# Fourth layer of a four-block transformer: key pieces ordered by VectorE and ScalarE in place of GpSimd

## The reference, cut to what matters

```
# layers 1 to 3:  scores[b,h,n,m] = q[b,h,n,:] . k[b,h,m,:]         (over tokens)
# layer 4:        attn = einsum('nthd,ntkd->nthk', q * scale, k)     (over heads, for each token)
#                 out  = einsum('nthk,ntkd->nthd', softmax(attn), v)
#                 out  = out.transpose(0, 2, 1, 3).reshape(n, t, d)
```

## Time and profile before

| | us |
|---|---|
| median of the three timed runs | 1486.37 |
| the profiled execution | 1485.1 |
| its span in the profile | 1483.4 |
| PE busy in the span | 1256.1 |
| DVE busy | 1121.3 |
| ACT busy | 935.5 |
| POOL busy | 325.4 |

### The profile page before, as it was taken

How to read it: one execution, slowest core, us unless ns; L and a number is a source line. 1 busy time by engine, 2 the same in 40 slices (tenths; PEclk the granted TensorE clock), 3 DMA queues, 4 the chain that set the end, 5 groups by cost and what they waited for, 6 DMA issues and landing times.

```text
span 1483.4 us, 36868 instructions
## 1 busy us (share of the span) xinstructions
PE 1256.1 (85%) x13282; PEld 808.8 (55%) x13314; DVE 1121.3 (76%) x2839; ACT 935.5 (63%) x2107; POOL 325.4 (22%) x446
## 2 busy tenths in 40 slices
PE   6365779888869999999999999999878898888886
PEld 4122335655446666666666666666645565656654
DVE  3844668877778888888888888888868888897642
ACT  0032456657637777777777777777657777776763
POOL 2000111111122222222222222222233343333301
PEclk9996688999979999999999999999989999999998
DMA  6304444234424444444444454444599999999900
GB/s 183 102 0 105 114 107 111 74 72 120 115 75 116 126 128 126 126 125 127 124 125 126 125 127 124 126 124 126 122 94 130 96 124 137 143 136 114 89 26 24
DMA packets 198481, 163.63 MB, mean 110 GB/s; under 512 B 80136, under 2 KB 182480, under 8 KB 192160
## 3 DMA queue, kind: packets, MB, share of 16 engines
q1 hardware_dynamic: 189920, 153.60, 54.5%
q10 hardware_dynamic: 8384, 7.69, 1.8%
HBM read 98.05 MB, written 62.41 MB: 108 GB/s over the span
## 4 chain that ended last, share of the span: by engine, by line
PE 36%; DVE 20%; DMA 12%; ACT 11%; issue 11%; SPq 6%; ACTq 3%; another core or an unknown queue 0%; DVEq 0%; POOL 0%; POOLq 0%
PE lin L1515 7%; PE lin L1531 6%; DMA norm_room<-stack_dram 5%; DMA stack_room<-stack_dram 4%; DVE maxima L1120 4%; PE o_bank L1468 4%; ACT hT_last L713 3%; PE score_bank L1406 3%; ACT p_room L732 3%; PE score_bank L1362 2%; PE st_bank L1437 2%; ACT h2T L718 2%; ACT h1T L718 2%; DVE gated L1178 2%; SPq L421 2%
## 5 line engine op out<-in xcount | busy, mean ns | idle before, releaser
L1120 DVE TENSOR_REDUCE maxima<-score_bank 128x4 f32<-128x512 f32 x512 | 329.1, 684 | 109.1 <-PE score_bank L1406 107.6
L732 ACT ACTIVATE p_room<-st_bank 128x512 f32<-128x512 f32 x512 | 276.9, 598 | 117.5 <-PE st_bank L1437 87.9
L616 POOL TENSOR_TENSOR part_low<-qk_rest,part_mid 96x512 bf16<-96x512 f32 x96 | 111.2, 1158 | 405.5 <-DVE part_mid L1103 405.5
L1531 PE MATMUL lin<-w_f,gelu 128*128 128x144 f32 (+1 forms) x1280 | 181.2, 299 | 3.8 <-ACT max_T L815 2.5
L1531 PEld LDWEIGHTS lin<-w_f,gelu 128*128 128x128 f32 (+1 forms) x1280 | 171.6, 201 | 7.3 <-ACT max_T L815 3.7
L1515 PE MATMUL lin<-h2T,w_h 128*128 128x512 f32 (+1 forms) x320 | 170.6, 632 | 4.4 <-ACT h2T L718 2.6
L1406 PE MATMUL score_bank<-stack_room 62*128 62x128 bf16 x2048 | 104.5, 223 | 77.3 <-DMA stack_room<-stack_dram 34.1
L1468 PE MATMUL o_bank<-p_room,v_room 128*32 128x128 f32 x4096 | 168.0, 282 | 0.4 <-issue 0.4
L607 POOL TENSOR_TENSOR x<-x,gated 128x288 f32<-128x288 f32 x64 | 53.9, 843 | 417.7 <-DVE gated L1178 417.7
L848 ACT ACTIVATE gelu<-lin 128x512 f32<-128x512 f32 (+1 forms) x160 | 90.9, 589 | 83.3 <-PE lin L1519 76.5
L1406 PEld LDWEIGHTS score_bank<-stack_room 62*128 62x128 bf16 x2048 | 59.8, 96 | 149.7 <-issue 47.2
(11 more groups left out here) (194 smaller groups left out, 2434.7 us busy)
## 6 DMA issues: line engine op xcount, KB each, us to landing
stack_room<-stack_dram SPq DMA_DIRECT2D x96, 512.0 KB, 8.4
stack_dram<-part_high SPq DMA_DIRECT2D x64, 288.0 KB
gates<-gates_dram SPq DMA_DIRECT2D x64, 288.0 KB, 3.3
norm_room<-stack_dram SPq DMA_DIRECT2D x32, 512.0 KB, 9.6
stack_dram<-part_mid SPq DMA_DIRECT2D x64, 192.0 KB
stack_dram<-part_high SPq DMA_DIRECT2D x64, 144.0 KB
stack_dram<-part_mid SPq DMA_DIRECT2D x64, 96.0 KB
stack_dram<-part_low SPq DMA_DIRECT2D x64, 96.0 KB
```

Of the source, the lines that this page charges most:

```text
L616: eng.tensor_tensor(part_low[:, T, :], qk_rest[:, T, :], part_mid[:, T, :], ALU.subtract)\
L732: eng.activation(probs[:, i % PBUFS, :], st_bank[i % 2][:, :], ACT.Exp, scale=float(HD) ** -0.5)\
L1120: eng.tensor_reduce(maxima[:, b, CH * c:CH * c + CH], bank_of(f"S{i}")[:, :].rearrange("p (h k) -> p h k", h=CH), AX_X, ALU.max)\
L1531: ins = eng.matmul(o, gelu[0:k, T, b * TOK:(b + 1) * TOK], w_f2[l][0:k, T, :], start=T == 0, stop=T == FCT - 1)
```

## The change

POOL's `order_keys` goes, with its four calls. DVE gets one with two calls, ACT one with two calls, and the one semaphore `ordered_k` becomes two: `ordered_k_even` (DVE: pieces 0, 1, 4, 5) and `ordered_k_odd` (ACT: pieces 2, 3, 6, 7). The copies have the same shapes and addresses as before. `load_stack(L)` waits for both semaphores in place of the one; `scores` waits for the one that its pair needs. The order of queries is as before.

```
 load_stack (SP):
-                need(eng, "ordered_k", L - 1, PIECES - 1)
+                need(eng, "ordered_k_even", L - 1, PIECES // 2 - 1)
+                need(eng, "ordered_k_odd", L - 1, PIECES // 2 - 1)
 POOL: def order_keys removed, and in body:
                 mods_of(M, 0)
-                order_keys(J, 0)
                 rstd_of(M, 0)
-                order_keys(J, 1)
                 add_mlp(Q, 0)
                 rstd_of(P, 1)
-                order_keys(J, 2)
-                order_keys(J, 3)
                 add_mlp(Q, 1)
 ACT:
+            def order_keys(g, b):
+                if not flow_is(g, "t"):
+                    return
+                need(eng, "stack_loaded", g, STACK_LOADS - 1)
+                if b == 1:
+                    need(eng, "st_done", g - 2, STEPS - 1)
+                for k in (2 * b, 2 * b + 1):
+                    out_piece, in_piece = piece_of(g, 1, k)
+                    eng.activation(out_piece, in_piece, ACT.Copy).then_inc(S["ordered_k_odd"], 1)
...
                 copy_max(g, 3)
+                order_keys(J, 1)
                 exponentials(g, 4)
...
                 copy_max(J, 1)
+                order_keys(J, 3)
 DVE:
+            def order_keys(g, b):
+                if not flow_is(g, "t"):
+                    return
+                need(eng, "stack_loaded", g, STACK_LOADS - 1)
+                if b == 0:
+                    need(eng, "st_done", g - 2, STEPS - 1)
+                for k in (2 * b, 2 * b + 1):
+                    eng.tensor_copy(*piece_of(g, 1, k)).then_inc(S["ordered_k_even"], 1)
...
                 maxima_of(g, 6)
                 statistics(M, 0)
+                order_keys(J, 0)
                 maxima_of(g, 7)
...
                 if not late:
                     statistics(P, 1)
+                order_keys(J, 2)
                 maxima_of(J, 2)
 scores (PE):
-                    need(eng, "ordered_k", g, pair + 1)
+                    need(eng, ("ordered_k_even", "ordered_k_odd")[pair // 2 % 2], g, pair // 4 * 2 + 1)
```

More of the change, by code:

```diff
@@ L167 @@
     "mods1": 2, "mods2": 2,
-    "v_mixed": 4, "ordered_q": PIECES // 2, "ordered_q_late": PIECES // 2, "ordered_k": PIECES,
+    "v_mixed": 4, "ordered_q": PIECES // 2, "ordered_q_late": PIECES // 2, "ordered_k_even": PIECES // 2, "ordered_k_odd": PIECES // 2,
     "qk_rest": QKT, "qk_sq": QKT, "norm_done": 1, "norm_max": 1, "norm_ln": 1, "norm_exp": 1, "norm_y2": 1, "norm_t": 1,
@@ L177 @@
                  "v_stored": GB, "v_loaded": 1}
-TOKEN_ONLY = {"v_mixed", "ordered_q", "ordered_q_late", "ordered_k", "v_stored", "v_loaded"}
+TOKEN_ONLY = {"v_mixed", "ordered_q", "ordered_q_late", "ordered_k_even", "ordered_k_odd", "v_stored", "v_loaded"}
 FIRST_TOKEN_GROUP = FLOW.index("t") * GROUPS
@@ L617, in low @@
                    .then_inc(S["qk_low"], 1)
[L619 to L627, removed]
             eng.wait_ge(setup["mods_kept"], 2 * LAYERS + 1)
```

## The result

The changed kernel took 1498.94 us (median of four runs, 1495.53 to 1502.29); the kernel before, 1485.32 (1479.63 to 1487.57). The ratio is 1.0097, 95% interval [1.0055, 1.014]: slower, by about half as much as forecast. The time lies inside the range (1497 to 1526), but outside the forecast's own 1505 to 1517 and near the time of rival B (1501). The profiled execution has a span of 1493.8 us against 1483.4, so +10.4 of the 25.5 that were forecast for it.

The account below looks back on a forecast made before the run. Bound: the fourth layer's loop of load landing, body's work, staging buffer free, next load. Five turns 17.5, first 5.9, sixth 0.3, tail 1.8 make 25.5 us on 1485.1, so 1510.6, stated as 1511; range 1497 to 1526.

Parts of the forecast that it names:

- rival B: Fourth-layer turns: PE and ACT shorten the way after the landing to 26 or less; turns +1.5 us, 1501; chance 0.18.
- The wait of load_stack: SP's stack load: waits for ACT's last key copies behind copy_max(J, 1), so issued 5.9 us later in body 23.
- The way from landing to copy_max(J, 1): Fourth-layer body, from DVE's start on the landed load to copy_max's end: 27.1 us against 29.7 before.
- Rival A: Head of the body: DVE is the bound and POOL's copies its brake; 16 us less, 1470; chance 0.06.
- The load's own time: Stack load, from first issue to DVE's start on what it brought: taken as 16.0 us, as before.
- The clock: PE's wait at scores(g, 7): low clock catches one turn in three more often, +0.5 us a turn.
- rival C: Every turn: low clock, and v stores slowing the load's tail; 11 us more, 1522; chance 0.20.
- First turn, +5.9: Body 23: its way gains nothing, so the later load is paid in full, +5.9 us.
- Sixth turn, +0.3: Turn without the work of new groups: later load +4.8 us, less about 4.5 won back, +0.3.
- Tail, +1.8: Body 30, where no load follows: the delay by ACT's second pair of copies stays, +1.8 us.

Follow-up runs that it names:

- e2: The changed kernel with ACT's order_keys(J, 3) moved from the body's end to ahead of exponentials(g, 7); 1475.9 us, ratio 0.9969.
- e1: The kernel before, all keys on POOL, with load_stack(L) also waiting for the first two exponentials of group J; 1501.4 us, ratio 1.0143.
- e6: The changed kernel plus eight unused POOL copies in each fourth-layer body, at the old places of its key copies; 1505.9 us, ratio 1.0191.
- e8: The kernel before with the even key pairs moved to DVE, odd pairs still on POOL, none on ACT; 1469.2 us, ratio 0.9947.
- e3: The changed kernel with SP waiting for all ordered pieces before the gates' load, putting it right ahead of the stack load; 1517.2 us, ratio 1.024.
- e7: The changed kernel with only the gates' load moved behind the stack load; 1497.3 us, ratio 1.0129.

## Why the prediction was right or wrong

**The wait of load_stack: right.** The load was issued 2.03 us after `copy_max(J, 1)` ended (2.2 forecast), directly after ACT's last copy. e2, with the same work, removes the loss by moving the pair, and e1 shows that a late load alone costs what the change costs. Two of the signs that the prediction named were missed: DVE's waits for the landing came to 30.6 us (35 or more forecast), and the turns to 43.3 (45 to 46).

**The way from landing to copy_max(J, 1): the number right, partly by luck.** It is 27.1 us, the forecast value. But the terms written down for it give 27.5, or 26.4 if the second pair of copies is covered, and not 27.1. The 29.7 that it was compared with is the mean of the five bodies from 1171.20 on, the last of them by the wrong landing of 1339.63; in the five full turns it was 30.0. Of the 2.9 us that went, e1 loses 0.9 (29.1) with POOL's copies still in place, from the late load alone. That fits rival B's mechanism. The rest is POOL's brake, as e1 and e6 (28.5, idle copies) show. Rival A had a true mechanism, but with the late load it could only pay part of the bill. With the late load gone it is small: e2 and e8 end at 0.9969 and 0.9947.

**The load's own time: wrong, the term that was mis-sized.** "An issue that comes later is a landing that comes later" took 16.0 us over unchanged. The five turns measured 14.2. The prediction had the reason in its rows: the gates' load was issued 0.5 us ahead of the stack load, and I read that pair only for who waits for whom. Once ACT holds the stack load, the gates' 288 KB stand 6 us ahead of it. e3 puts them right ahead again, and the 1.5 us return. Five turns at 27.1 + 2.0 + 14.2 = 43.3 are +1.1 a turn where +3.5 was forecast; the load makes 1.8 of that difference, the clock 0.5.

**The clock: wrong for this kernel.** 0.5 us a turn was added for more falls, with PE standing about 3 us before `scores(g, 7)`. PE stood there only 0.8 to 1.8 us in the five turns, and the granted clock was 1.00 in four of them, as in the kernel before. The likely reason is that ACT's last pair delays PE's work too; it was not tried by itself. In e1, which has no such pair, PE stood 2.2 to 4.9 us and the clock was below 1.00 in four of the five turns (in the turn shown, 0.70 over 1177 to 1180 and 0.66 over 1195 to 1200). In e3, with a still later landing, PE stood 2.5 to 4.8 us and the clock was below 1.00 in all five. So rival C's low clock is part of the time of these two kernels, but the changed kernel had no more of it than the kernel before. Two turns, e1 first: PE's wait (the last number), then the turn's row (us, busy us by engine, granted clock, DMA share, GB/s):

```profile
1177.89 0.40 PE L1407 MATMUL score_bank<-stack_room 62*128 62x128 bf16 x8 [2.51 <-DVE maxima L1121]
1174.56:1219.63 45.07, 39.80 (x458) 27.14 (x457) 36.24 (x86) 31.64 (x71) 16.66 (x19) 0.92 0.97 114
```

```profile
1178.39 0.40 PE L1418 MATMUL score_bank<-stack_room 62*128 62x128 bf16 x8 [0.85 <-DVE maxima L1120]
1175.94:1218.48 42.54, 36.58 (x457) 24.69 (x456) 34.65 (x91) 35.17 (x74) 8.73 (x11) 1.00 1.08 121
```

The prediction read in the Trainium skill, "TensorE: Matmul & The Clock Gate", section "HAM oscillation", that every turn would be caught. The kernel of that section waits for its DMA longer at each step than PE waited in the changed kernel, so it didn't say this of every wait. Rival C's other price, the v stores beside the load's tail, didn't show either, since the load became shorter.

**First turn, +5.9:** nearly right, +5.1; the load, 14.6 after 15.2, makes 0.6 of what is missing. **Sixth turn, +0.3:** measured -2.0, again the load (15.0 after 17.0). In e3 this load took 15.5, so here the gates' place explains only part. **Tail, +1.8:** measured +3.5. e2, whose ACT has no copies at the body's end, has 103.4 us from the last landing to the end, near the changed kernel's 103.9, so ACT's pair doesn't explain it. In the traces of the ten experiments this stretch is 101.9 to 106.7 us, so two traces can't settle a term of 1.8.

**Rival B** came out near its number, 1501, but only in small part by its mechanism: it let the way shrink to 26, and it was the load that shrank. That the time still lies in the stated range is owed to the room that the range left for B, and not to a term that foresaw the shorter load.

## What to carry to other kernels

When work moves from one engine to another, look first at where in the receiver's list it ends and which buffer it still holds there: two copies at the end of a body cost about 1% of the time more than the same two copies 5 us earlier (1.0097 against 0.9969). When a transfer is delayed, its duration is up for question too: read what was issued just ahead of it. And an engine with time to spare isn't free to use if it stretches its neighbour's instructions.

## What the runs showed of the hardware that was not expected

- In these kernels a DMA of 288 KB that broadcasts to 128 partitions, issued 0.5 us ahead of four loads of 512 KB, made these take 1.5 us longer (15.8 and 15.9 against 14.4 us from issue to landing, means of seven). About 1 us of it is in SP's four issues (6.3 and 6.2 against 5.1 us). Issued 2.4 us ahead (e2), the loads that can be read took 15.2 to 15.7 us. Issued 6 us ahead (changed) or behind (e7, 14.4 in the five turns) it cost nothing that shows. Why, the runs don't show.
- A small cast on VectorE took 0.88 us in place of 0.17 beside a GpSimd copy that touches other tiles (e6), while VectorE's reductions out of PSUM beside GpSimd's copies kept their 0.64 us each. The Trainium skill, "SBUF — State Buffer", section "two separate sides", describes an exclusive lock on the port pair that the two engines share; the 0.88 and the 0.64 agree with it.
- One copy of 128x512 bf16, gathered in steps of 64 bytes, took 0.6 us on VectorE and 1.05 to 1.1 on ScalarE and on GpSimd.
